# Forming the feed-forward's first operands inside the attention pass's last two slots

## The reference, cut to what matters

```python
x = _layernorm(x + autocorrelation(x))             # in effect 2x, normalised, unless a guard says otherwise
x = _layernorm(x + xattn(ctx, ctx, x))             # softmax(ctx @ x.T / 16, axis=1) @ ctx, per batch
x = _layernorm(x + x @ W_base.T + moe_lora(x))     # 4096 x 2048 rows by 2048 x 2048, 8 experts of rank 8, top 2
```

## Time and profile before

| | us |
|---|---|
| median of 3 runs (lowest, highest) | 1966.44 (1965.95, 1971.0) |
| the profiled execution, its own time | 1964.43 |
| its span, first to last instruction | 1962.6 |
| PE busy | 1779.3 (91%) |
| DVE busy | 1361.5 (69%) |
| ACT busy | 791.6 (40%) |
| mean granted clock of TensorE | 0.973 |

### The profile page before, as it was taken

One profiled execution on the slowest core, in us unless ns is written; L12 is line 12 of the kernel. 1 busy time (PEld: TensorE's weight loads), 2 busy tenths in 40 slices (PEclk: granted clock), 3 DMA queues, 4 the chain that ended last, 5 costly groups with the idle time before them and its releaser, 6 DMA issues. The chain is left out here.

```text
span 1962.6 us, 27015 instructions
## 1 busy us (share of the span) xinstructions
PE 1779.3 (91%) x10194; PEld 953.8 (49%) x10210; DVE 1361.5 (69%) x2605; ACT 791.6 (40%) x939; POOL 200.1 (10%) x358
## 2 busy tenths in 40 slices
PE   3989999999853959999999999998899999999997
PEld 2656665767531425445544445443344444444443
DVE  3878888888859866777666777799654655565463
ACT  5888888788745211222222212133231222213111
POOL 1223232323200000000000000000010010010000
PEclk9999999999975989999999999999999999999998
DMA  8899999999758499999999999945999879988882
GB/s 279 196 278 269 287 249 288 269 282 257 223 199 239 113 240 254 269 255 236 247 256 266 250 227 227 231 164 161 294 259 253 274 221 259 266 249 252 248 242 108
DMA packets 565563, 472.70 MB, mean 241 GB/s; under 512 B 498416, under 2 KB 502512, under 8 KB 544624
## 3 DMA queue, kind: packets, MB, share of 16 engines
q1 hardware_dynamic: 565424, 470.87, 87.8%
HBM read 237.51 MB, written 109.58 MB: 177 GB/s over the span
## 5 line engine op out<-in xcount | busy, mean ns | idle before, releaser
L1558 PE MATMUL bank_f<-w_hi_f,a_cols_f 128*128 128x512 f16 x3584 | 1090.4, 381 | 78.0 <-DVE w_lo_f L1292 36.4
L1558 PE MATMUL bank_f<-w_lo_f,a_cols_f 128*128 128x512 f16 x1792 | 683.6, 381 | 0.0
L1558 PEld LDWEIGHTS bank_f<-w_hi_f,a_cols_f 128*128 128x128 f16 x3584 | 352.2, 98 | 507.4 <-DMA a_cols_f<-rows_f 41.7
L1148 ACT ACTIVATE rows_f<-xn_f 128x1024 f16<-128x1024 f32 x78 | 82.4, 1057 | 500.1 <-DMA xn_f<-x_scratch 337.8
L1558 PEld LDWEIGHTS bank_f<-w_lo_f,a_cols_f 128*128 128x128 f16 x1792 | 176.0, 98 | 204.0 <-issue 3.2
L1323 DVE SCALAR_TENSOR_TENSOR y_f<-bank_f,w_iscale_f,y_f 128x512 f32<-128x512 f32 x192 | 134.5, 742 | 169.3 <-PE bank_f L1558 169.2
L649 PE MATMUL ps_s_fast<-k_both_fast,q_hi_fast 128*128 128x256 f16 x1024 | 170.8, 275 | 7.4 <-DMA k_both_fast<-v_lo_fast 6.4
L1284 DVE TENSOR_TENSOR rows_f<-xn_f,rows_f 128x1024 f16<-128x1024 f32 x78 | 94.3, 1209 | 97.6 <-ACT rows_f L1148 97.6
L1323 DVE SCALAR_TENSOR_TENSOR y_f<-bank_f,w_iscale,y_f 128x512 f32<-128x512 f32 x192 | 134.7, 743 | 34.8 <-PE bank_f L1558 31.6
L1284 DVE TENSOR_TENSOR rows_f<-sums_f,rows_f 128x1024 f16<-128x1024 f32 x63 | 76.8, 1219 | 114.8 <-ACT rows_f L1148 114.6
L1148 ACT ACTIVATE rows_f<-sums_f 128x1024 f16<-128x1024 f32 x63 | 66.3, 1052 | 195.9 <-DMA a_cols_f<-rows_f 193.3
(11 more groups left out here) (210 smaller groups left out, 2300.8 us busy)
## 6 DMA issues: line engine op xcount, KB each, us to landing
xbuf_fast<-x SPq DMA_DIRECT2D x32, 1024.0 KB, 7.8
x_scratch<-x2buf_fast SPq DMA_DIRECT2D x32, 1024.0 KB, 5.7
y_f<-x_scratch SPq DMA_DIRECT2D x32, 1024.0 KB, 7.8
xn_f<-x_scratch SPq DMA_DIRECT2D x62, 512.0 KB, 4.9
kept_scratch<-a_cols_f SPq DMA_DIRECT2D x45, 512.0 KB, 3.4
xn<-x_scratch SPq DMA_DIRECT2D x45, 512.0 KB, 6.8
a_cols_f<-kept_scratch SPq DMA_DIRECT2D x45, 512.0 KB, 8.7
cbuf<-ctx_in SPq DMA_DIRECT2D x16, 1024.0 KB, 5.9
```

The costliest lines, as they stand in the source:

```text
L1148: nc.scalar.activation(rows[g % 2][:, 0], source(i), ACT.Copy).then_inc(a_hi, 1)
L1558: ins = nc.tensor.matmul(bank[i][:], a_cols[:, i, part + kk, :], ww[:, W_SLOT[i], kk, :], start=(kk == 0 and part == 0 and ww is w_hi), st ...
```

## The change

The seven items of the first pair are formed by the attention pass. In slot 14 SP reloads the first 256 rows of x2 into the two context buffers `cbuf` (free by then); ACT and DVE form high parts, sums and low parts of items 0 to 5 in slot 14 and finish item 6 in slot 15, into four places in a free key buffer; SP turns each into one of six column buffers (two new ones and the free halves of q_lo and q_hi) and stores it to device memory: items 4 to 6 to the place of the kept operands, items 0 to 3 to a new scratch. The feed-forward loads all seven with plain transfers, and its own forming, turning and keeping of the first pair is taken out. The loads of ag_raw and of weight unit 0 at the attention's end now also wait until all seven items have their low parts, and the load of the first rows of x2 is dropped. Some semaphores are merged.

```diff
+                def load_first():
+
+                    for r in (1, 0):
+                        sp.wait_ge(vlo_done, R * (nb - 1) + r + 1)
+                        sp.wait_ge(stored[0][r], 16 * (base + 1))
+                        sp.dma_start(cbuf[r][:], x2_out[r * P:(r + 1) * P, :]).then_inc(c_loaded[r], 16)
+
+                def turn_first(i):
+
+                    sp.wait_ge(f_lo, i + 1)
+                    if i >= len(f_cols):
+                        sp.wait_ge(f_stored, 16 * i - 16)
+                    elif i >= 2:
+                        sp.wait_ge(sim_done, R * nb)
+                        sp.wait_ge(folded, R * nb)
+                    sp.dma_start_transpose(f_cols[i % len(f_cols)], f_rows[i % 4].rearrange("p a c -> p (a c)")).then_inc(f_turned[i % 2], 16)
+
+                def store_first(i):
+
+                    sp.wait_ge(f_turned[i % 2], 16 * (i // 2 + 1))
+                    sp.dma_start(first_items[i], f_cols[i % len(f_cols)]).then_inc(f_stored, 16)
+
                 def slot(n, half, parity):
+                    if n == nb - 2:
+                        load_first()
+                    if n == nb - 1:
+                        turn_first(3)
+                        store_first(2)
...
+                    if n == nb - 2:
+                        turn_first(0)
+                        turn_first(1)
+                        store_first(0)
+                        turn_first(2)
+                        store_first(1)
+                    if n == nb - 1:
+                        for i in range(4, NM):
+                            turn_first(i)
+                            store_first(i - 1)
+                        store_first(NM - 1)
 
                 batch_slots(sp, None, nb, slot, 0)
 
-                sp.wait_ge(stored[0][0], 16)
-                sp.wait_ge(w_squared, 2 * W_TILES)
-                sp.dma_start(consts["xn0"][:], x2_out[0:P, :]).then_inc(prefetched, 16)
                 sp.wait_ge(fwd_done, 4 * nb)
-                sp.wait_ge(vlo_done, R * nb)
-                sp.dma_start(consts["ag_raw"][:], ag_in.rearrange("p k c -> p (k c)")).then_inc(prefetched, 16)
-                sp.dma_start(consts["cbuf0"][:], w_chunks[0]).then_inc(prefetched, 16)
+                sp.wait_ge(f_lo, NM)
+                sp.dma_start(consts["ag_raw"][:], ag_in.rearrange("p k c -> p (k c)")).then_inc(tables_loaded, 16)
+                sp.dma_start(consts["cbuf0"][:], w_chunks[0]).then_inc(tables_loaded, 16)
                 store(nb - 1, (nb - 1) % 2)
...
+                sp.wait_ge(f_stored, 16 * NM)
...
+                    def first_high(i):
+
+                        if i < 2:
+                            f_loaded(act, (A22, A11)[i])
+                        else:
+                            act.wait_ge(f_sum, i - 1)
+                        if i == 0:
+                            act.wait_ge(sim_done, R * (nb - 1))
+                        if i >= 4:
+                            act.wait_ge(f_turned[i % 2], 16 * (i // 2 - 1))
+                        nc.scalar.activation(f_rows[i % 4][:, 0], f_source(i), ACT.Copy).then_inc(f_hi, 1)
...
                     for j in range(CG):
                         emptied_bank(j)
                         if j == 1 and is_batch(n - 1, nb):
                             spread2(n - 1, other, 1)
+                        if j == 2 and n == nb - 1:
+                            first_high(NM - 1)
...
                     normalise1(0)
+                    first_highs(0, 1, 2)
                     softmax_exp(0)
+                    first_highs(3)
                     square_weights(0)
                     square_weights(1)
                     guard_squares(0)
                     guard_squares(1)
                     softmax_exp(1)
+                    first_highs(4)
                     guard_squares(2)
                     guard_squares(3)
+                    first_highs(5)
...
                     for j in range(CG):
                         emptied_bank(j)
+                        if j == 2 and n == nb - 1:
+                            first_low(NM - 1)
...
                     value_low(0)
+                    if n == nb - 2:
+                        first_low(0)
+                        first_sum(2)
+                        first_low(1)
                     softmax_max(0)
                     fold(0)
                     fold(1)
                     x_stats(1)
+                    if n == nb - 2:
+                        first_sum(3)
+                        first_low(2)
                     softmax_norm(0)
+                    if n == nb - 2:
+                        first_low(3)
+                        first_sum(4)
                     softmax_max(1)
                     value_low(1)
+                    if n == nb - 2:
+                        first_low(4)
                     softmax_norm(1)
+                    if n == nb - 2:
+                        first_sum(5)
+                        first_low(5)
+                        first_sum(6)
...
         def forms(s, i):
 
-            return makes(s) and (s < NP_ or i not in KEPT)
+            return makes(s) and s and (s < NP_ or i not in KEPT)
...
                 wait_stored(sp, x2_stored, NP_)
-                load_block(0, A22)
-                load_block(0, A21)
                 load_unit(1)
+                for i in range(NM):
+                    sp.dma_start(whole(i), first_items[i]).then_inc(kept_loaded[0], 16)
                 load_unit(2)
-                turn(0, 0)
-                turn(0, 1)
-                load_unit(3)
-                turn(0, 2)
-                turn(0, 3)
-                load_unit(4)
-                turn(0, 4)
-                turn(0, 5)
                 for b in (A22, A21):
                     load_block(1, b)
+                load_unit(3)
+                load_b(0)
+                load_unit(4)
                 load_unit(5)
-                turn(0, 6)
-                load_b(0)
                 load_residual(0)
                 load_unit(6)
-                keep(0, 4)
-                keep(0, 5)
                 load_unit(7)
...
                 def wait_slot(s, i):
 
+                    if s == 0:
+                        pe.wait_ge(kept_loaded[0], 16 * NM)
+                        return
```

More of the change, by code:

```diff
@@ L50 @@
 HALF = L // 2
+A11, A12, A21, A22 = range(4)
+OPERANDS = [(A22,), (A11,), (A21, A11, ALU.subtract), (A21, A22, ALU.add), (A12, A22, ALU.subtract), (A11, A22, ALU.add),
+            (A11, A12, ALU.add)]
+KEPT = (4, 5, 6)
 def after(eng, sem, value):
@@ L154, in attention_pass @@
         ones = sb("ones", [P, P], F32)
+        k_free = k_both[nb % 2][:].rearrange("p k t c -> p (k t c)")
+        f_rows = [k_free[:, i * L:(i + 1) * L].rearrange("p (a c) -> p a c", a=2) for i in range(4)]
+        f_sums = [consts["xn0"][:, 0:HALF], consts["xn0"][:, HALF:L]]
+        f_cols = [sb(f"f_cols{i}", [P, KT, P], F16)[:] for i in range(2)] + [q[:, :, i * P:(i + 1) * P] for q in (q_lo, q_hi) for i in range(2)]
         w_sumsq = sb("w_sumsq", [P, 2 * (L // P + 1)], F32)
@@ L486, in context_scale, with first_sum, first_low @@
                             v.tensor_scalar(lscale[parity][:], iscale[parity][:], C ** -0.5, None, ALU.mult).then_inc(scale_ready, 1)
+                    def first_sum(i):
+                        one, two, op = OPERANDS[i]
+                        for b in (one, two):
+                            f_loaded(dve, b)
+                        if i == 2:
+                            dve.wait_ge(w_squared, 2 * W_TILES)
+                        else:
+                            dve.wait_ge(f_sum, i - 2)
+                        if i >= 5:
+                            dve.wait_ge(f_lo, 1 if i == 5 else 3)
+                        v.tensor_tensor(f_source(i), f_block(one), f_block(two), op).then_inc(f_sum, 1)
+                    def first_low(i):
+                        dve.wait_ge(f_hi, i + 1)
+                        v.tensor_tensor(f_rows[i % 4][:, 1], f_source(i), f_rows[i % 4][:, 0], ALU.subtract).then_inc(f_lo, 1)
                     for j in range(CG):
                         emptied_bank(j)
+                        if j == 2 and n == nb - 1:
+                            first_low(NM - 1)
                         if cur:
@@ L492, in slot @@
                             if b == 0:
-                                after(dve, stored[parity][r], 16 * half)
+                                after(dve, stored[parity][r], 16 * (base + half))
                             dve.wait_ge(context_done, CG * n + j + 1)
@@ L665, in slot @@
                             pe.wait_ge(w_summed, 4)
-                            nc.tensor.matmul(verdict_all, ones[:], verdict[:], start=True, stop=True).then_inc(w_reduced, 1)
+                            nc.tensor.matmul(verdict_all, ones[:], verdict[:], start=True, stop=True).then_inc(w_summed, 1)
                         if j == CG - 1 and n != -1:
@@ L1203, in _ @@
                 wait_stored(act, x2_stored, NP_)
[L1204 removed]
```

(8 more changed lines are left out.)

74 lines of the change are left out of this document (31 added, 43 removed).

## The result

The changed kernel is slower by about half a per cent: median 1978.46 us (1975.83 to 1984.5) against 1967.33 (1965.95 to 1971.17) for the kernel before, ratio 1.0054 with a 95% interval of 1.0041 to 1.0067. The forecast was "about the same", within 0.3%, and about 1970; what came is the slower rival. Its 1977 is what the ratio gives on the prediction's own scale (1966.44 x 1.0054 = 1977.1, inside the range of 1960 to 1978, at its edge); the median as measured, 1978.46, lies 0.5 above the range. The profiled execution took 1975.83, its span is 1974.0 against 1962.6, so 11.4 us are to be found between the two traces.

What follows compares the result with a forecast made beforehand. DVE was taken to pace the feed-forward's opening, the seam being TensorE's one deep hole. Terms +18.9 - 14.6 - 0.5 = +3.8 gave 1968.2 us for the profiled execution, 1970 on the median's scale; range 1960 to 1978.

Steps and rivals of the forecast that it cites:

- about the same: Whole kernel: the forecast chosen, a time within +-5.9 us (+-0.3%) of the kernel before; chance 0.52.
- the slower rival: Whole kernel: same mechanism with crowded landings in the queue, +10.7 us, 1977; chance 0.35.
- Part 1 and 2: Feed-forward's opening: removed DVE work and a hole give -18.5 us, a new stall +3.9; sum -14.6.
- the hole before the scores: DVE's 4.92 us idle before the scores in the feed-forward's opening, said to go as operands load early.
- the stall at unit 2: Feed-forward's opening: DVE waits for weight unit 2, loaded behind the items; 3.9 us, bounds 2.1 to 6.5.
- Part 3: Attention's last two slots, 14 and 15: inserted DVE and ACT work makes the last normalisation later, +6.1 us.
- Part 4: SP's queue at the attention's end: waits and final transfers start the feed-forward at 597.2 instead of 578.31, +18.9 us.
- The chain: SP's in-order queue: after batch 14's store, turn 4, store 4 and turn 6 each wait for the landing before.
- the hand-overs: Three landings waited for in SP's queue: 5.3, 4.9 and 5.0 us, together 15.2; alone 12.7, crowded 17.7.
- The burst: Final 4.26 MB (item 6, ag_raw, weight unit 0, batch 15's stores): 13.8 us at 375 GB/s, last landing 595.3.
- rule and row: Transposes: skill page's 350 to 400 GB/s, sum 1.6 us less, against the profile's 237; the profile row was followed.
- Part 5: After the first sweep: three stores of kept operands leave the feed-forward's queue, worth 0 to 1.5 us; -0.5 taken.

Runs made afterwards that it cites:

- the better order: Changed kernel with items 4 and 5 turned, and items 3 and 4 stored, ahead of batch 14's store in SP's queue; ratio 1.0016 to the kernel before.

## Where the prediction was right, and the term that failed

The forecast was +3.8 and "about the same" within 0.3%; measured were +11.4 between the traces and a ratio of 1.0054 (from 1.0041), so the gain and the loss don't cancel. That the result still falls at the edge of the stated range is owed to the range, which took in nearly all terms at their worst. The parts compare as follows.

**Part 1 and 2 (the feed-forward's opening, -14.6): right.** Measured -15.1; update 0 is 70.0 after DVE's start where 70.5 was said, the hole before the scores is gone, the stall at unit 2 is 2.59 (3.9 said, 2.1 to 6.5 as bounds; 2.08 to 3.42 in the other traces with this feed-forward), and no second unit is waited for. PE's wait for operands ended 14.5 after DVE's start (15.2 said):

```profile
615.87 0.59 PE L1645 MATMUL bank_f<-w_hi_f,a_cols_f 128*128 128x512 f16 x1 [43.26 <-DMA a_cols_f<-kept_scratch]
```

**Part 3 (slots 14 and 15, +6.1): right.** The row maximum is at 553.17 (552.7 said), the first context addition at 562.34 (562.3), the last normalisation at 577.38 (576.6). Of each measured time 0.8 is there before the added work; without it the last normalisation is at 576.6, as said. On ACT, batch 14's second spread and normalisation are where the walk had put them:

```profile
559.90 1.99 ACT L450 ACTIVATE junk_fast<-x2buf_fast,nmean_fast 128x2048 bf16<-128x2048 f32 x1
...
563.62 2.09 ACT L456 ACTIVATE x2buf_fast<-x2buf_fast,nb_fast,rs_fast 128x2048 f32<-128x2048 f32 x1
```

**Part 4 (SP's queue, +18.9): the term that was mis-sized.** The chain was drawn right, and its start fits (turn 4 issued at 566.50, 566.2 said). But DVE's first weight unit began at 601.40 instead of 597.2: +23.1, at the upper bound (23.1). What failed is the price of the hand-overs, "I take 5.3, 4.9 and 5.0", 15.2 in sum and 17.7 when crowded. From the issue of turn 4 to the last store of an item (585.41, 581.5 said) 18.9 passed, and SP's rows above show where. The first hand-over took 10.3 instead of 5.3: the store of item 4 went out at 576.81. Turn 4 landed 7.4 after its issue, later than the longest landing used (6.3), and SP wasn't free then: the store of item 3 and turn 5 stand between turn 4 and the store of item 4 in its order, and the issues of the two turns alone took 4.50 and 4.27. The prediction had item 5 beside the chain in the queue, but not in SP's order on the chain. The other two hand-overs were shorter than said (4.2 and 4.4 instead of 4.9 and 5.0). The burst behind them was right in sum, 16.0 from the last item's store to DVE's first unit where 13.8 + 1.9 = 15.7 was said, though it ran at 330 GB/s (585.4 to 599.5) and not at 375.

So the prediction priced a hand-over by its *landing*, as if the queue and SP were free in between. The runs show that the queue itself is full: in the better order the DMA share is between 0.92 and 1.13 in each 5 us from 545 to 590, and still the gap is 17.46. Eleven transfers of 0.52 MB (seven transposes, four stores of slices) move in pieces of 256 bytes: 5.77 MB, by estimate 27 us of queue time at 215 GB/s and 14 at 410.

That also settles the weighing of rule and row for the transposes. The page Advanced Engine Details and Errata of the Trainium skill, section X-Bar Transpose (TRN2), has them as fast as regular transfers. It nearly holds against regular transfers of which four in seven have pieces of the same 256 bytes (ratio 1.0016 against 1.0010), and not against ones with whole rows (1.0003 against 0.9970). With transposes alone in flight the engines are full (share 1.12) at 212 GB/s.

**Part 5 (after the first sweep, -0.5): wrong in this pair of traces.** The shift grows from +8.0 at update 0 to +11.4 at the end. Whether this belongs to the change stays open. In every experiment the shift against the kernel before grows, too, from update 0 to the end, by 0.5 with only the feed-forward changed, by 3.4 with only the attention pass changed (whose feed-forward is the old one), and in the others by 0.1 to 5.3. No run isolates it.

**The rival.** "The queue, not the work" was given 0.35, 1977 us, and the condition that the feed-forward begins later than about 599.3. It began at 601.40, and crowded hand-overs are the reason, more crowded than its 17.7. The rest of its split was less exact: the stall at unit 2 was short, the burst no longer than said, and part of its total is the growth of part 5, which it didn't have. The rows that spoke for it stood in the prediction already (237 GB/s at a share of 1.19 with transposes in flight); they should have priced the seven transposes, and did not, because a landing of 5.3 says when a transfer is over and not how much of the queue it has used up.

## What to carry to other kernels

A stage that is idle on DVE may be full on the DMA engines, and moved work must be priced on every one of them: here 13.6 us of DVE time were moved out of a stage bound by DVE and took with them, by the estimate above, some 27 us of queue time (transposes and four stores) into the 45 us before a barrier. An in-order issuing engine belongs to the same count: what stands between two links of a chain in its list is on the chain. Price a transfer in a crowded stretch by its bytes over the rate that its piece size gets at a full share, not by its landing in an empty one. And before rejecting such a move, try a part of it and look at the layout: four of seven items, turned and stored in a better order, fitted at no cost to the attention pass, and a one-line change of where the columns lie shortened the gap by 2 to 3 us.

## What was not expected of the hardware

Transfers with 256-byte pieces fill the engines at about 215 GB/s (at a share of 0.89), from SBUF to SBUF too as far as the mixed stretch tells, about half of the 404 to 410 GB/s of whole 4 KB rows, and transposing transfers behave like them (212 at 1.12). The issue of a transpose on SP, 1.92 us where the queue had run dry, takes 4.27 and 4.50 where it is full, so the engine that issues is held up too. The packets by size show it without any timing. Between 540 and 595, with transposes and with plain copies of whole rows in their place:

```profile
DMA packets 16482, 13.57 MB, mean 247 GB/s; under 512 B 14773, under 2 KB 14773, under 8 KB 15797
```

```profile
DMA packets 3396, 15.71 MB, mean 286 GB/s; under 512 B 367, under 2 KB 367, under 8 KB 2615
```
